# A fourth output buffer, turned quarters and a last store in four parts, in a depthwise convolution on TensorE

## What is computed

```python
ch = x.shape[-1]
k = jnp.transpose(kernel, (1, 2, 0))[:, :, None, :]
y = lax.conv_general_dilated(x, k, window_strides=(1, 1), padding='SAME',
                             dimension_numbers=('NHWC', 'HWIO', 'NHWC'), feature_group_count=ch)
return x + y
```

## Time and profile before

| | before |
|---|---|
| median of 3 runs | 781.43 us (781.16 to 782.96) |
| the profiled execution | 781.88 us |
| its span, first to last instruction | 780.1 us |
| mean granted TensorE clock | 0.999 of full speed |
| TensorE busy | 764.4 us (98%) |
| VectorE busy | 732.9 us (94%) |
| ScalarE busy | 680.0 us (87%) |
| GpSimd busy | 434.6 us (56%) |
| DMA | 304.39 MB, mean 390 GB/s |

### The profile page before, as it was taken

How to read it: one execution, slowest core, us unless ns; L and a number is a source line. 1 busy time by engine, 2 the same in 40 slices (tenths; PEclk the granted TensorE clock), 3 DMA queues, 4 the chain that set the end, 5 groups by cost and what they waited for, 6 DMA issues and landing times.

```text
span 780.1 us, 19014 instructions
## 1 busy us (share of the span) xinstructions
PE 764.4 (98%) x6528; PEld 762.7 (98%) x6528; DVE 732.9 (94%) x2116; ACT 680.0 (87%) x1726; POOL 434.6 (56%) x464
## 2 busy tenths in 40 slices
PE   6999999999999999999999999999999999999997
PEld 6999999999999999999999999999999999999997
DVE  5999999999999999999999999999999999989996
ACT  6798898888898989898898989898988998988985
POOL 6646557475554554554647555566556574745651
PEclk9999999999999999999999999999999999999999
DMA  9999999999999999999999999999999999999975
GB/s 361 421 414 372 412 366 419 399 389 406 392 402 403 405 386 411 382 410 387 402 380 404 401 397 392 403 375 412 380 405 377 413 404 394 389 403 368 416 315 241
DMA packets 28751, 304.39 MB, mean 390 GB/s; under 512 B 3184, under 2 KB 3312, under 8 KB 4208
## 3 DMA queue, kind: packets, MB, share of 16 engines
q1 hardware_dynamic: 28656, 303.19, 98.0%
HBM read 153.75 MB, written 149.42 MB: 389 GB/s over the span
## 4 chain that ended last, share of the span: by engine, by line
PE 79%; DMA 8%; DVE 8%; ACT 2%; issue 1%; SPq 0%; DVEq 0%; ACTq 0%
PE sums L399 26%; PE sums L405 23%; PE sums L406 23%; PE sums L402 8%; DMA y<-y_out 7%; DVE x_low L344 5%; DVE y_out L355 3%; DMA x_in<-x 1%; ACT x_high L311 1%; ACT y_out L318 1%; SPq L231 0%; SPq L233 0%; SPq L227 0%; DVEq L146 0%; DVEq L352 0%
## 5 line engine op out<-in xcount | busy, mean ns | idle before, releaser
L399 PE MATMUL sums<-matrix,x_low 126*128 126x208 f32 (+5 forms) x2304 | 629.9, 273 | 10.1 <-POOL matrix L288 7.7
L288 POOL TENSOR_TENSOR matrix<-spread,mask 127x270 fp32r<-127x270 f32 x384 | 377.1, 1012 | 321.8 <-PE sums L406 264.2
L405 PE MATMUL sums<-matrix,x_high 126*128 126x208 f32 (+4 forms) x1920 | 530.6, 276 | 0.0
L406 PE MATMUL sums<-matrix,x_high 126*128 126x208 f32 (+4 forms) x1920 | 530.6, 276 | 0.0
L318 ACT ACTIVATE y_out<-sums 128x270 f32<-128x270 f32 (+6 forms) x1152 | 412.3, 405 | 87.1 <-DMA y<-y_out 42.2
L399 PEld LDWEIGHTS sums<-matrix,x_low 126*128 126x128 f32 (+1 forms) x2304 | 443.2, 192 | 11.7 <-POOL matrix L288 7.7
L355 DVE TENSOR_TENSOR y_out<-sums,y_out 128x176 f32<-128x176 f32 (+2 forms) x1728 | 396.3, 273 | 36.1 <-ACT y_out L318 8.7
L344 DVE TENSOR_TENSOR x_low<-x_in,x_high 128x768 fp32r<-128x768 f32 x384 | 398.7, 1039 | 5.7 <-ACT x_high L311 5.7
L405 PEld LDWEIGHTS sums<-matrix,x_high 126*128 126x128 f32 (+1 forms) x1920 | 369.6, 193 | 0.0
L406 PEld LDWEIGHTS sums<-matrix,x_high 126*128 126x128 f32 (+1 forms) x1920 | 369.2, 192 | 0.0
L311 ACT ACTIVATE x_high<-x_in 128x768 fp32r<-128x768 f32 x384 | 327.7, 853 | 6.9 <-DMA x_in<-x 6.8
(11 more groups left out here) (6 smaller groups left out, 0.7 us busy)
## 6 DMA issues: line engine op xcount, KB each, us to landing
x_in<-x SPq DMA_DIRECT2D x95, 1536.0 KB, 10.1
y<-y_out SPq DMA_DIRECT2D x95, 1520.0 KB, 12.9
rest<-later SPq DMA_DIRECT2D x1, 2300.0 KB, 13.9
x_in<-x SPq DMA_DIRECT2D x4, 384.0 KB, 4.8
y<-y_out SPq DMA_DIRECT2D x1, 832.5 KB, 4.2
y<-y_out SPq DMA_DIRECT2D x1, 687.5 KB, 5.7
mask<-masks SPq DMA_DIRECT2D x1, 270.0 KB, 3.6
first<-consts SPq DMA_DIRECT2D x1, 125.0 KB, 2.1
```

The costliest lines, as they stand in the source:

```text
L288: pool.tensor_tensor(matrix[c % SLOTS][kind][0:whole, part, :].rearrange("p (b d q) -> p b d q", d=TAPS, q=COLS), spread[c % SLOTS][kind][ ...
L399: pe.matmul(target, low, turned[:, HIGH], start=tile is bank["tiles"][0], stop=False, skip_group_check=True)
L405: pe.matmul(target, high, turned[:, LOW], start=False, stop=False, skip_group_check=True)
L406: product = pe.matmul(target, high, turned[:, HIGH], start=False, stop=last, skip_group_check=True)
```

## The change

Three things are changed. `Y_SLOTS` goes from 3 to 4, with one more buffer, semaphore and memset. The quarters are turned: the kinds are TALL, FLAT, TALL, FLAT, their coordinates along and across stay, so the plane's walk is the mirror image in the diagonal (upper left, lower left, lower right, upper right); GpSimd makes the TALL products first (`ORDER`), and TensorE's wait for them goes by the quarter in place of the kind. The last channel is stored in four parts: rows 29 to 54 after 9 banks' adds, rows 0 to 6 after 10, rows 7 to 15 after 11, rows 16 to 28 after all 12. The last lines of the diff write the centre pixel's place in its tile as constants of the same value.

```diff
--- before.py
+++ after.py
@@ -20,12 +20,13 @@
 CENTRE = SIDE // 2
 FLAT, TALL = range(2)
 KINDS = 2
+ORDER = (TALL, FLAT)
 
 QUARTERS = (
-    (FLAT, (0, 14), (0, 9, 18)),
-    (TALL, (0, 14), (28, 37, 46)),
-    (FLAT, (27, 41), (28, 37, 46)),
-    (TALL, (27, 41), (0, 9, 18)),
+    (TALL, (0, 14), (0, 9, 18)),
+    (FLAT, (0, 14), (28, 37, 46)),
+    (TALL, (27, 41), (28, 37, 46)),
+    (FLAT, (27, 41), (0, 9, 18)),
 )
 PER_BANK, PER_QUARTER = 2, 6
 TILE_COUNT = len(QUARTERS) * PER_QUARTER
@@ -50,7 +51,7 @@
 
 X_SLOTS = 4
 SLOTS = 2
-Y_SLOTS = 3
+Y_SLOTS = 4
 GROUP = 4
 GROUPS = CHANNELS // GROUP
 TURNED = KINDS * FILTER
@@ -139,7 +140,8 @@
 ADDS = plan_of_sums(PLAN)
 BANK_COUNT = len(PLAN)
 ADDS_BEFORE = [sum(len(b["adds"]) for b in PLAN[:n]) for n in range(BANK_COUNT + 1)]
-TOP_BANKS, TOP_ROWS = 6, min(b["rows"][0] for b in PLAN[6:])
+LAST_STORES = [(9, PLAN[2]["rows"][1] - 1, SIDE), (10, 0, PLAN[10]["rows"][0]),
+               (11, PLAN[10]["rows"][0], PLAN[11]["rows"][0]), (12, PLAN[11]["rows"][0], PLAN[2]["rows"][1] - 1)]
 
 
 def build(nc, consts, masks, later, x, out):
@@ -241,12 +243,12 @@
                 if c:
                     store_y(c - 1)
             c = CHANNELS - 1
-            split = SIDE * TOP_ROWS
-            for t, done, end in ((TOP_BANKS, 0, split), (BANK_COUNT, split, OUT_COLS)):
+            for t, top, bottom in LAST_STORES:
+                done, end = SIDE * top, SIDE * bottom if bottom < SIDE else OUT_COLS
                 sp.wait_ge(added, ADDS * c + ADDS_BEFORE[t])
                 sp.dma_start(out[c, :, done:end], y_out[c % Y_SLOTS][:, done:end]).then_inc(y_stored[c % Y_SLOTS], 16)
             for slot in range(Y_SLOTS):
-                count = len(range(slot, CHANNELS, Y_SLOTS)) + (c % Y_SLOTS == slot)
+                count = len(range(slot, CHANNELS, Y_SLOTS)) + (len(LAST_STORES) - 1) * (c % Y_SLOTS == slot)
                 sp.wait_ge(y_stored[slot], 16 * count)
 
         @block.gpsimd
@@ -282,7 +284,7 @@
                     pool.wait_ge(masks_loaded, 16)
                 if c >= SLOTS:
                     pool.wait_ge(sums_done, BANK_COUNT * (c - SLOTS + 1))
-                for kind in range(KINDS):
+                for kind in ORDER:
                     shape = [whole, ROWS // TAPS, TAPS, COLS]
                     for part in (HIGH, LOW):
                         pool.tensor_tensor(
@@ -384,7 +386,7 @@
                     kind, quarter = bank["kind"], bank["quarter"]
                     if t % (BANK_COUNT // PIECES) == 0:
                         if quarter < KINDS:
-                            pe.wait_ge(matrix_step, 2 * KINDS * c + 2 * (kind + 1))
+                            pe.wait_ge(matrix_step, 2 * KINDS * c + 2 * (quarter + 1))
                         pe.wait_ge(low_ready, PIECES * c + quarter + 1)
                     wait_bank(c, t)
                     for tile in bank["tiles"]:
@@ -431,13 +433,12 @@
 def lay_out_taps(taps):
 
     step = np.arange(TAPS).reshape(1, -1)
-    _, top, left = list(corners_of_tiles())[CENTRE_TILE]
     turned = np.zeros((P, CHANNELS, KINDS, FILTER), taps.dtype)
     centre = np.zeros((P, KINDS, FILTER), taps.dtype)
     masks = np.zeros((P, KINDS, CELLS), taps.dtype)
     pixels = PIXELS + 1
     v, u = np.divmod(np.arange(PIXELS), LONG)
-    v, u = np.append(v, CENTRE - top).reshape(-1, 1), np.append(u, CENTRE - left).reshape(-1, 1)
+    v, u = np.append(v, SHORT).reshape(-1, 1), np.append(u, LONG - 1).reshape(-1, 1)
     a, b = (TAPS - 1 - (step - v) % TAPS)[:, :, None], (TAPS - 1 - (step - u) % TAPS)[:, None, :]
     r, q = np.arange(ROWS).reshape(1, -1), np.arange(COLS).reshape(1, -1)
     down, over = (r >= v) & (r < v + TAPS), (q >= u) & (q < u + TAPS)
```

## The result

| | before | changed |
|---|---|---|
| median | 781.43 us | 777.77 us |
| executions beside each other (5 each) | 780.80 to 783.36 | 777.34 to 778.11 |
| profiled execution | 781.88 us | 777.77 us |
| span | 780.1 us | 776.2 us |
| waits of bank 0's copy on stores | 42.2 us in 48 channels | none |

The ratio of changed to before is 0.9928, with a 95% interval of 0.9901 to 0.9955: faster by 0.45 to 0.99%. The medians alone give 0.9953. The forecast time was 778.0 us, and its ratio to 781.43 was 0.9956, just outside that interval.

What follows compares the result with a forecast made beforehand. TensorE was taken as the floor, 7.907 us a channel. 7.70 us before the first matmul + 759.07 floor + 3.69 loss + 5.74 tail = 776.2 us span; with 1.78 outside it, 778.0 us, range 776.6 to 780.2.

Steps and rivals of the forecast that it cites:

- The mechanism: ScalarE's copy of bank 0 waits for an output slot, VectorE gets late, and TensorE loses time some channels on.
- Which losses go: Of 7.60 us TensorE loss, 3.69 us in channels 0 to 3 stay; 3.91 us in later channels go.
- the tail's term: End of the span, 774.36 to 780.1 us: 5.74 us, kept unchanged in the sum.
- Sum: 1.20 + 1.01 + 1.70 = 3.91 us: Fourth slot's gain: losses of channel 4, of channels 5 to 11 and of channels 63 to 95 all go.
- The DMA queue as cover: DMA engines bear the higher pace, or landing grows from 12.9 to 16.8 us, still under 20.4: cost zero.
- The other bound: DMA queue: 396 GB/s is all the engines give, costing 3.9 us, all the gain.
- Quarters turned at 0: Copies and adds swap orientation in every channel; bank sizes for matmuls and copies stay, orientation shows no price: 0 us.
- Four parts at 0: Last channel's stores: finer cutting gains nothing, as the DMA block still ends at 778.3; 0 us, bounds +0.5 and -0.5.
- Rival (a): Tail shortens too, by 1.2 us, as the last store moves 366 KB, not 852 KB: 776.8 us; chance 0.09.
- Rival (b): Most gain isn't collected: 396 GB/s is the limit, or VectorE stays late after channel 3; say 780.2 us; chance 0.18.
- Rival (c): Slower: GpSimd's products meet VectorE's x_low again and again, 0.5 us in each 4 channels from 7 on: 789 us; chance 0.05.
- Rival (d): The waits weren't the slot's, so the 7.60 us loss stays: 781.4 to 781.9 us; chance 0.04.

Runs made afterwards that it cites:

- the later GpSimd: Kernel before, GpSimd's products for channel c held until TensorE has finished bank 2 of channel c - 1: 791.57 us with three slots, 787.99 us with four.

## Why the prediction was right, and where it was wrong

**The mechanism: right.** The slot's wait was the cause. It goes with a fourth slot (777.16 alone), it stays without (781.83), and it goes too, all but the wait in channel 3, when the stores land 0.8 us sooner (778.10).

**Which losses go: right.** 3.69 us of channels 0 to 3 were to stay; 3.82 are there. Channels 4 to 95 were to take 7.907 us each; they do. The span was to be 776.2 and is 776.2. That it is exact is in part luck: the tail's term was kept at its old size, and in it 0.5 us gained by the earlier last full store stand against 0.3 lost by the four parts.

**The step that failed: what before costs.** The sum was made against one profiled execution, with 7.60 us lost, and its saving of 3.91 us was then set against a median of three. But the loss varies from one execution to the next. A store takes about as long as three slots allow, so it differs how many waits are long and whether VectorE falls into its late phase. In all groups together the kernel before gave 54 times from 777.8 to 788.0 us, median 783.1; the three groups of the experiments had medians of 783.84, 781.30 and 784.06. Kernels of the same body with four or five slots gave 28 times from 776.75 to 778.21. The term that failed is therefore the last one of the fourth slot, "Sum: 1.20 + 1.01 + 1.70 = 3.91 us", taken as the kernel's loss where it was one execution's: measured, it goes from nothing in the fastest execution of before to some 10 us in the slowest, about 5.3 at the median (783.1 - 777.8), 0.7% instead of 0.44%. The sign of it was on the page: the earlier trace rows put the median landing, 12.9 us, at the very 12.5 that are allowed, and three executions were 1.8 us apart. I used the closeness to explain the waits and not to ask how they vary. That the spread comes from the waits on stores is shown by what takes it away: one number, the slots, turns 778.43 to 788.16 us into 777.34 to 778.11, and shorter stores do the same with three slots (777.37 to 778.18). What a slow execution looks like inside is argued from the profiles at 781.49 and 781.88 us; none of the slowest was profiled.

**The DMA queue as cover: right, for a reason I hadn't settled.** The other bound (396 GB/s is the limit) is out: 411 GB/s cost nothing, and the limit lies from 414 to 423. The landing didn't grow by the 3.9 us that I allowed either, but stayed at 13.0.

**Quarters turned at 0: right.** The turned kernel with three slots stands at 0.9992 of the one before, within some 2 us; the closer pair is 777.40 turned and 777.16 not, beside each other. The two paces of the floor, 0.6 us apart in 92 channels, occur in both orders.

**Four parts at 0: wrong by 0.3 us.** The reasoning on the block held (first part's data at 770.75, with the queue empty for 0.65 us ahead of it, so that the first part is what sets the end). But I took the block's rate as the same for small pieces, and it fell from 413 to 388 GB/s. It is less than the 0.5 us bound. **Rival (a)** is out: the last piece of 357.5 KB took 3.8 us to land, and the 832.5 KB piece of the kernel with the slot alone 3.7, so size made no difference to the last piece. By the rule of the Trainium skill ("DMA: Bandwidth & Descriptors", Anatomy of one DMA), a fit for one DMA issued from GpSimd, the two would differ by an estimated 1.1 us; the trace doesn't agree for these, which SyncE issued behind others.

**Rival (b)** is out: no late round after channel 3. **Rival (c)** didn't occur in the changed kernel: its third x_low comes ahead of GpSimd's products after channel 2, and its fourth, which meets them in every channel and takes 1.2 us, costs TensorE nothing. Its price of 0.5 us a time is real in the three-slot profiles, as the eight channels above show; the later GpSimd doesn't bear on it, since a wait of its own comes in. **Rival (d)** is out.

**What stays open:** how much of the loss needs GpSimd, as I read the earlier trace rows. The eight slow third pieces, each with a long channel behind it, fit that reading, and the six long channels without one show that it isn't the only way. But this is an order of events and not an experiment: the kernel that was to separate them added a wait of its own.

## What to carry to other kernels

When a buffer comes free about as late as it is wanted, the cost is a distribution and not a number: work out what the slots allow, compare it with the median and the longest landing, and price the change against several executions and not one profile. One more slot, or a few per cent less traffic, takes the spread away with the wait. And a last store cut finer need not help: here the block of stores began with its first part either way, and two parts were better than four.

## What the runs showed of the hardware

The DMA share doesn't tell how full the DMA engines are. Over the middle of the run (60 to 740 us) it reads 0.99 to 1.01 at 366, 397, 411 and 419 GB/s alike, and only in the last of these runs does the queue hold up every channel. What tells is the landing of the stores: 12.1, 13.1 and 13.7 us in the first three, 22.8 in the last, where the slots stopped it. So most of a landing of 12 us isn't a queue that comes and goes with the traffic, as I had read it, since it hardly falls when 8% of the traffic is taken away; what it is made of stays open. And SyncE's issue of a DMA took 0.33 us in most rows, but 0.74 to 0.76 and 0.91 to 0.97 for the last two of the four parts in four profiles; a few of the full stores took up to 1.1 us as well.
